# Latent attention's first weights loaded during the ternary feed-forward, its rotary exchange moved to VectorE, and the gated ternary work re-timed

## What is computed

```python
# ternary feed-forward: w -> clip(round(w / mean|w|), -1, 1)
h = gelu(x @ w1q.T + b1, approximate=False);  y = h @ w2q.T + b2
# latent attention
q = (x @ wq).reshape(b, s, H, NOPE + ROPE)      # 128 plain + 64 rotary channels a head
ckv = x @ wkv_a                                 # 128 latent channels + 64 rotary ones
q_pe, k_pe = rope(q_pe), rope(k_pe)             # re = xe*cos - xo*sin; ro = xo*cos + xe*sin
kv = (c @ wkv_b);  k = [k_nope, k_pe];  o = softmax(causal(q k^T / sqrt(192))) v
return o @ wo
# gated feed-forward, weights in bf16, groups of 64 (used two stages later)
scale = max(mean|w_g|, 1e-8);  w_hat = clip(round(w_g / scale), -1, 1) * scale
w_used = w + (w_hat - w)
```

## Time and profile before

| what | value |
|---|---|
| median of 3 runs | 2308.65 us |
| profiled execution, its own time | 2316.98 us |
| its span in the trace | 2315.2 us |
| mean granted clock of TensorE | 0.978 |
| stage of latent attention, from barrier to end | 1367.6 to 1778.9 us |

### The profile page before, as it was taken

One profiled execution on the slowest core, in us unless ns is written; L12 is line 12 of the kernel. 1 busy time (PEld: TensorE's weight loads), 2 busy tenths in 40 slices (PEclk: granted clock), 3 DMA queues, 4 the chain that ended last, 5 costly groups with the idle time before them and its releaser, 6 DMA issues. The chain is left out here.

```text
span 2315.2 us, 35594 instructions
## 1 busy us (share of the span) xinstructions
PE 2182.3 (94%) x13410; PEld 1720.5 (74%) x13410; DVE 1444.6 (62%) x3965; ACT 1172.8 (51%) x3016; POOL 465.4 (20%) x383
## 2 busy tenths in 40 slices
PE   9998999999999999999977988999899998997998
PEld 5645788888888888888866965665655884665987
DVE  2385777787778777777657435454555456883535
ACT  2153767676767676766543424453443445771222
POOL 1210212221222212221111002223232000220533
PEclk9999999999999999999998999999999998998999
DMA  6013111100111111100003023213212310003100
GB/s 243 7 64 112 37 35 38 38 16 30 37 38 38 36 36 38 37 10 26 10 1 146 1 76 123 100 64 127 80 76 99 137 52 20 2 2 147 71 1 29
DMA packets 44772, 131.94 MB, mean 57 GB/s; under 512 B 6535, under 2 KB 21671, under 8 KB 40119
## 3 DMA queue, kind: packets, MB, share of 16 engines
q1 hardware_dynamic: 32792, 108.59, 12.8%
q0 software_dynamic: 2304, 12.58, 1.3%
q10 hardware_dynamic: 9504, 8.50, 1.2%
HBM read 109.10 MB, written 20.15 MB: 56 GB/s over the span
## 5 line engine op out<-in xcount | busy, mean ns | idle before, releaser
L782 PE MATMUL psum<-qa_kv_raw,context 128*128 128x256 f32 (+1 forms) x1536 | 343.6, 380 | 0.0
L782 PEld LDWEIGHTS psum<-qa_kv_raw,context 128*128 128x128 f32 (+1 forms) x1536 | 277.2, 184 | 44.9
L768 PE MATMUL psum<-qa_w,qa_xq 128*100 128x256 bf16 (+1 forms) x3072 | 267.0, 247 | 3.1 <-PEq L60 3.1
L768 PEld LDWEIGHTS psum<-qa_w,qa_xq 128*100 128x100 bf16 x3072 | 256.1, 126 | 4.1 <-issue 4.0
L884 ACT ACTIVATE qa_prob<-psum,qa_nm 100x361 f32<-100x361 f32 x128 | 72.0, 562 | 168.3 <-DVE qa_nm L1016 168.3
L2473 ACT ACTIVATE it_prob<-psum,it_nm 100x257 f32<-100x257 f32 (+1 forms) x256 | 101.9, 412 | 42.0 <-DVE it_nm L2497 41.8
L839 PE MATMUL psum<-qa_catq,qa_o 128*128 128x400 f32 x512 | 111.9, 361 | 9.9 <-DVE X L1055 6.0
L1108 POOL TENSOR_TENSOR qa_w<-qa_w_raw,qa_w 128x768 bf16<-128x768 f32 x28 | 46.0, 1643 | 371.0 <-DVE qa_w L958 371.0
L978 DVE BATCH_NORM_STATS2 qa_st<-psum 100x6 f32<-100x128 f32 x320 | 69.7, 284 | 78.7 <-PE psum L768 78.7
L1114 POOL TENSOR_TENSOR qa_o<-qa_o_raw,qa_o 128x512 fp32r<-128x512 f32 x32 | 40.6, 1270 | 350.5 <-DVE qa_o L966 350.5
L1007 DVE TENSOR_SCALAR qa_nrm_t<-psum,qa_mv,qa_sd 100x128 f32<-100x128 f32 x320 | 107.9, 404 | 2.4
(11 more groups left out here) (355 smaller groups left out, 5013.6 us busy)
## 6 DMA issues: line engine op xcount, KB each, us to landing
qa_w_raw<-in_qa_w SPq DMA_DIRECT2D x8, 1536.0 KB, 6.7
la_gf_raw<-in_gf_w SPq DMA_DIRECT2D x16, 768.0 KB, 4.4
gf_w<-gf_ternary SPq DMA_DIRECT2D x4, 3072.0 KB, 25.4
qa_piece<-in_tf_pieces ACTq DMA_DIRECT2D x64, 128.0 KB, 2.1
qa_o_raw<-in_qa_o SPq DMA_DIRECT2D x8, 1024.0 KB, 5.1
gf_ternary<-la_gf_made POOLq DMA_DIRECT2D x8, 768.0 KB, 3.6
gf_ternary<-gf_last_made POOLq DMA_DIRECT2D x8, 768.0 KB, 3.6
context<-in_context SPq DMA_DIRECT2D x8, 722.0 KB, 12.4
```

The costliest lines, as they stand in the source:

```text
L768: mm = pe.matmul(psum[0:T, 2 + at // 512, at % 512:at % 512 + width], xq[:, kind, k, b * T:(b + 1) * T], w3[:, s, part, k, at:at + width], ...
L782: mm = pe.matmul(psum[0:rows, i // 2, (i % 2) * 256:(i % 2) * 256 + 256], ctxT[:, k, b * TC + t0:b * TC + t0 + rows], kv_raw[:, s, k, :], ...
```

## The change

1. The ternary stage's `raws` hold two quarters, not four; SP loads quarters 2 and 3 when the blocks of quarters 0 and 1 have been made. Behind them, still in this stage, SP issues the latent stage's first four loads (`LatentEarly.fetch`) into buffers that live on their own.
2. The exchange of the rotary halves is done by DVE: `turn` multiplies by cosine in one instruction and by sine in four, each of 32 partitions, reading one block of 32 and writing its neighbour; the sum becomes a difference of two SBUF tensors. `neg_swap`, the swap units and the third block of `w_a` are gone. A quad has 12 units, and rot units come at 0, 2, 6 and 8. Keys turn in the same way.
3. Set 0 and set 1 are summed and made ternary earlier in the units, and `take_scale` comes behind the unit of its own sum.
4. Joins: `join_values(0)` comes ahead of the scores, 1 and 2 behind the first two scores, 3 in batch 1, keys in batches 2 to 5. At the start keys use banks 6 and 7 in turn, the waits on the first units are spread, and the transposes come before the keys.
5. POOL does each of its two steps in three instructions of 512 columns.
6. ACT loads its table of the exponential in the units. The image and text stage uses `w_qt`, `both` and `Y` again instead of tensors of its own.

```diff
+def fetch_ternary_quarter(sp, q, raws, raw_in, a):
+    cols, rows = slice(q * F // 4, (q + 1) * F // 4), slice(q * FC // 4, (q + 1) * FC // 4)
+    sp.dma_start(raws[0][:, q % 2], a["tf_up"][:, :, cols]).then_inc(raw_in[q], 16)
+    sp.dma_start(raws[1][:, q % 2], a["tf_down"][:, rows, :]).then_inc(raw_in[q], 16)
...
-            fetch_ternary_weights(sp, raws, raw_in, a)
+            for q in range(4):
+                if q >= 2:
+                    sp.wait_ge(S_["w_ready"], (q - 1) * FC // 4)
+                fetch_ternary_quarter(sp, q, raws, raw_in, a)
+            early.fetch(sp, a)
...
+    def fetch(self, sp, a):
+        sp.dma_start(self.w_a, a["la_a"]).then_inc(self.wa_in, 16)
+        sp.dma_start(self.w_qt[:, :, :], a["la_qt"][0]).then_inc(self.keys_in, 16)
+        sp.dma_start(self.w_kt[:, :, :], a["la_kt"][0]).then_inc(self.keys_in, 16)
+        sp.dma_start(self.w_rot, a["la_rot"][0]).then_inc(self.wrot_in, 16)
...
-    prepare = {0: 0, 4: 1, 10: 2}
-    sum_after = {2: (0, 0), 4: (0, 1), 6: (0, 2), 8: (1, 0), 10: (1, 1), 12: (1, 2), 14: (2, 0)}
+    prepare = {0: 0, 2: 1, 8: 2}
+    sum_after = {2: (0, 0), 3: (0, 1), 4: (0, 2), 5: (1, 0), 6: (1, 1), 7: (1, 2), 11: (2, 0)}
     sum_beside = {1: (2, 1), 4: (2, 2)}
-    scale_after = {q + 1: xy for q, xy in sum_after.items()}
-    make_after = {7: 0, 13: 1}
+    make_after = {4: 0, 7: 1}
+    EXP_TABLE_AFTER = 9
...
-            units += [("q", i, half), ("rot" if i < 2 else "swap", i % 2, half)]
-    takes_out = {"q": "act", "rot": "dve", "swap": "dve"}
+            units += ([("rot", i, half)] if i < 2 else []) + [("q", i, half)]
+    takes_out = {"q": "act", "rot": "dve"}
...
-            for i in range(3):
+            for i in range(2):
...
+                pe.wait_ge(S_["values_in"], 32 * g + 32)
+                join_values(0, g * 8 + 4)
                 pe.wait_ge(S_["act"], g * per_quad["act"] + per_quad["act"])
-                pe.wait_ge(S_["dve"], g * per_quad["dve"] + per_quad["dve"])
+                pe.wait_ge(S_["qrot_ready"], g * per_quad["dve"] + per_quad["dve"])
...
+            def turn(raw, i, done):
+                dve.tensor_tensor(by_batch(by_cos[:, i, :]), by_batch(raw), four(cos), ALU.mult).then_inc(S_["turned"], 1)
+                for r0 in range(0, P, ROPE // 2):
+                    to, at = slice(r0, r0 + ROPE // 2), slice(r0 ^ ROPE // 2, (r0 ^ ROPE // 2) + ROPE // 2)
+                    last = dve.tensor_tensor(by_batch(by_sin[to, i, :]), by_batch(raw[at]),
+                                             sin[at, :].unsqueeze(1).broadcast_to([ROPE // 2, 4, T]), ALU.mult)
+                    last.then_inc(done, 1)
...
-                pool.tensor_tensor(diff[:, :, :], what[r][:, :, :], gw[r][:, :, :], ALU.subtract).then_inc(S_["diff_ready"], 1)
+                for y in range(3):
+                    last = pool.tensor_tensor(diff[:, y, :], what[r][:, y, :], gw[r][:, y, :], ALU.subtract)
+                last.then_inc(S_["diff_ready"], 1)
```

More of the change, by code:

```diff
@@ L1155, in before, with ternary_ffn_stage @@
     return (g, s, b - lag, n - lag) if b >= lag else (g - 1, 1 - s, b - lag + B, n - lag)
[L1162 to L1170, removed]
+def fetch_ternary_quarter(sp, q, raws, raw_in, a):
+    cols, rows = slice(q * F // 4, (q + 1) * F // 4), slice(q * FC // 4, (q + 1) * FC // 4)
+    sp.dma_start(raws[0][:, q % 2], a["tf_up"][:, :, cols]).then_inc(raw_in[q], 16)
+    sp.dma_start(raws[1][:, q % 2], a["tf_down"][:, rows, :]).then_inc(raw_in[q], 16)
+def ternary_ffn_stage(nc, core, a, abs_sums, early):
     X, psum = core.X, core.psum
@@ L1647, with __init__ @@
 LA_SCALE = float(1.0 / np.sqrt(NOPE + ROPE))
+class LatentEarly:
+    def __init__(self, nc, ctx):
+        self.both = ctx.enter_context(nc.sbuf_tensor("la_w_both", [P, 2 * C * 2 * P], F32))
+        self.w_a, self.w_rot = (self.both[:, i * C * 2 * P:(i + 1) * C * 2 * P].rearrange("p (c o) -> p c o", c=C)
+                                for i in range(2))
+        self.w_qt = ctx.enter_context(nc.sbuf_tensor("la_w_qt", [P, 4, D], F32))
+        self.w_kt = ctx.enter_context(nc.sbuf_tensor("la_w_kt", [P, 4, LORA], F32))
+        self.wa_in, self.wrot_in, self.keys_in = (nc.alloc_semaphore(f"la_{n}") for n in ("wa_in", "wrot_in", "keys_in"))
+    def fetch(self, sp, a):
[3 more added lines that the diff above has]
+        sp.dma_start(self.w_rot, a["la_rot"][0]).then_inc(self.wrot_in, 16)
 class LastGated:
@@ L1726, in latent_attention_stage @@
             "diff_ready", "made_ready")}
+        S_.update(wa_in=early.wa_in, wrot_in=early.wrot_in, keys_in=early.keys_in)
+        core.held += [early.wa_in, early.wrot_in, early.keys_in]
         block = ctx.enter_context(nc.Block())
@@ L1842, in quad @@
                     if q >= RING:
                         e, count = taken(q - RING)
-                        pe.wait_ge(S_[e], g * per_quad[e] + count)
+                        pe.wait_ge(S_[e], (g * per_quad[e] + count) * (4 if e == "dve" else 1))
                     bank = q % RING
-                    if kind in ("q", "rot"):
-                        for k in range(C):
-                            mm = pe.matmul(psum[:, bank, 0:HALF], (w_q if kind == "q" else w_rot)[:, k, i * P:(i + 1) * P],
-                                           X[:, k, cols(h)], start=(k == 0), stop=(k == C - 1))
-                    else:
-                        pe.wait_ge(S_["dve"], unit_out(g, ("rot", i, h)))
-                        mm = pe.matmul(psum[:, bank, 0:HALF], neg_swap[:, :], by_sin[:, i, :], start=True, stop=True)
+                    for k in range(C):
+                        mm = pe.matmul(psum[:, bank, 0:HALF], (w_q if kind == "q" else w_rot)[:, k, i * P:(i + 1) * P],
+                                       X[:, k, cols(h)], start=(k == 0), stop=(k == C - 1))
@@ L1946, in quad @@
                         magnitude_and_sign(g, prepare[q])
+                    if q == EXP_TABLE_AFTER:
+                        act.activation(spare[:, 2:3], core.eps[1.0], ACT.Exp)
+                joined_values(0, g * 8 + 4)
                 exps(g, 0)
+                joined_values(1, g * 8 + 5)
                 for b in range(B):
@@ L2146, in sb @@
             return ctx.enter_context(nc.sbuf_tensor(f"itp_{name}", shape, dt))
-        w = [sb(f"w{i}", [P, C, D]) for i in range(3)]
+        w = [early.w_qt, sb("w_ki", [P, C, D]), sb("w_kt", [P, C, D])]
         ctxT = sb("context", [P, RING, C, TC])
-        sq, rms, std = sb("sq", [P, C, HALF]), sb("rms", [P, 2, HALF]), sb("std", [P, N])
+        sq = early.both[:, 0:C * HALF].rearrange("p (c t) -> p c t", c=C)
+        rms, std = sb("rms", [P, 2, HALF]), sb("std", [P, N])
         spare = sb("spare", [P, 1])
```

188 lines of the change are left out of this document (85 added, 103 removed).

## The result

The changed kernel takes 2306.45 us (median of 15 runs, 2304.84 to 2310.55), the kernel before beside it 2309.88 (15 runs, 2306.97 to 2321.16): a ratio of 0.9976, 95% interval 0.9964 to 0.9987. It is faster, by 3.4 us where 16 were forecast, and so by less than the 0.5% bound.

What follows compares the result with a forecast made beforehand. TensorE, busy 94% of the span, was taken as the bound. Start 13.5, units 0.1 x 4, loops 1.05 and 1.1 made 16 us off the median 2308.65: 2293 us, own range 2287 to 2299, wide range 2279 to 2307.

Steps and rivals of the forecast that it cites:

- The start: Latent stage up to the first query unit: early loads, smaller w_a and shorter joins take 13.5 us off, between 11.5 and 14.
- 5.4 + 3.9: Start of the stage: 5.4 us off for w_a's 16 matmuls instead of 24, 3.9 off between first join and first unit.
- The units' waits: Query units: PE waits for DVE 1.65 and 2.1 us a quad; 38.5 us against 38.6, so the units give nothing.
- the meeting with POOL: Second wait of a quad: DVE's difference of two SBUF inputs is held by POOL's instruction, 0.55 us, bounds 0 and 1.17.
- units gain as well: Rival, query units: products follow after 0.49 and meet no POOL instruction, 5.8 us more off, 2287; without waits 2278; chance 0.20.
- The loops' sizes: Batch loops: seven joins instead of eight take 0.35 us off each of the first three quads, 1.1 off the fourth.
- the key joins cost little: Last two batches of the first three quads' loops: a chain of PE, ACT and DVE waits; 0.35 us off each quad.
- the term for the clock: Third quad's loop, 2.8 us over the second's by a clock fall and a POOL meeting: left even, nothing gained or lost.
- the clock eats it: Rival: eight gaps of about 2 us in four quads instead of four make the clock fall, 2302 to 2313; chance 0.22.
- the widest range given: Whole kernel: 2279 to 2307 us, leaving out the ends of the second and third rivals and the fourth.

Runs made afterwards that it cites:

- the experiment on the loads: The changed kernel with its four early loads issued at the head of the latent stage again, as before: 2310.57 us, ratio to the kernel before 0.9978.
- pool_whole: The changed kernel with GpSimd's two steps of each set in one piece again instead of three: 2316.52 us, ratio to the kernel before 1.0006.
- the clean base: The kernel before with two idle matmuls in PE's wait ahead of the scores of each quad: 2310.32 us, ratio to the kernel before 0.9975.
- the version with both edits: The changed kernel with take_scale ahead of the rot unit's products and key joins back in batches 4 to 7: 2274.8 us, ratio 0.983.
- keys late: The changed kernel with the key joins back in batches 4 to 7 of the loop: 2301.48 us, ratio to the kernel before 0.995.
- the experiment that keeps the waits and removes all falls in the stage but one: The changed kernel with idle matmuls ahead of both sums' waits (two, three) and key joins back in batches 4 to 7: 2296.31 us, ratio 0.9917.
- Fillers: The changed kernel with idle matmuls, two ahead of the sum behind unit 3, three ahead of that behind unit 7: 2303.6 us, ratio 0.9954.

## Why the prediction was wrong

**The start was right.** Forecast 13.5 us, measured 14.25: 4.78 to PE's first matmul (forecast 4.2; 4.2 by the idle time in the experiment on the loads, the rest is the stage before) and 9.47 from there to the first unit (5.4 + 3.9 = 9.3).

**The units' waits were right.** 1.65 and 2.1 us forecast, 1.67 and 2.0 (2.35 in the fourth quad) measured, released by L2000; 38.5 a quad forecast, 38.66 in the second. The 2.1 came out by two misses that cancel: the second wait was counted 0.15 short (1.5 beside 1.65, for the same chain) and the meeting with POOL 0.2 long. Products 0.57 long and 0.60 apart, and the difference longer by 0.35 where it met a third of POOL's (0.55 taken). The rule of "VectorE: DVE Perf Modes" in the Trainium skill (Two Vector instructions with no wait between them), that an instruction which starts in another quadrant than the last is held until the earlier ones have finished, agrees with the trace. So does pool_whole with the lock that "SBUF — State Buffer" (SBUF: two separate sides) in the Trainium skill describes: 2.56 us for 0.57. The rival *units gain as well* named the price of both waits together, 3.8 a quad; they were there, and it is the order of two instructions, not faster products, that took them away (4.0 a quad).

**The loops' sizes were right, the reasons in part.** Forecast 0.35 off in each of three and 1.1 in the fourth; measured against the clean base 0.44, -0.21, 0.44 and 0.55. The second and the fourth hold a fall; without it they are 0.44 (as the others) and 1.2 (29.97 to 28.75, the fourth loop of the version with both edits). The forecast counted the join that left and held that "the key joins cost little" in the last two batches. The joins of values were in fact worth 1.2 a loop (32.75 to 31.55, keys late), and the keys moved forward gave 0.76 of it back.

**The step that failed** is the term for the clock, put at nothing: "new gaps of 1.65 and 2.1 us are as good as the old one at making the clock fall. I leave it even". Even with what? The sum was read from a profile with two falls in the stage, of which the prediction saw one, and then taken off a median that is of the lower level. The kernel before with the filler, which lies at that level (2308.5 to 2311.0), has no fall from the first unit to the end of the stage; 6.5 us lie between its span and that of the profile. So there were no falls in the base that new ones could replace, and both traces of the changed kernel have them. Against the clean lengths they cost:

| where the clock falls | us |
|---|---|
| behind the second wait, first and third quad (1.64 + 1.69) | 3.3 |
| tail of the second loop (0.66) and its projection (2.31) | 3.0 |
| tail of the fourth loop (0.67) and its projection (2.3) | 3.0 |
| behind the gaps at 1767 and 1887 (1.7 + 0.7) | 2.4 |

That is 11.7 us of a miss of 2306.45 - 2293 = 13.5; most of the rest is the base, 2308.65, which lies 1.7 us under the median of the kernel with the filler (2310.32). Without the falls the changed kernel would take about 2306.45 - 11.7 = 2295 us, an estimate, and the experiment that keeps the waits and removes all falls in the stage but one takes 2296.3, with loops that are 2.3 us shorter (3 x 0.76). So the waits stand as forecast and the clock took the gain: the rival *the clock eats it*, which had 0.22, is what happened. Its price per fall, 1.75 to 2.8, nearly held: 1.65 behind a wait, 3.0 in a tail. What it missed is the place: of eight waits two brought a fall, and the larger part was lost in loop tails that the forecast had taken for harmless, and behind gaps after the stage that are as long in the kernel before and brought little or nothing there. That 2306.45 still lies inside the widest range given, 2279 to 2307, is owed to this rival and not to the sum.

**Left open:** why the clock falls at one of two equal gaps. In both traces of the changed kernel a wait of 2.0 us in the first quad and of 2.06 in the third brought a fall, one of 2.06 in the second and one of 2.35 in the fourth did not. With the keys late it was the first and the second quad, with the late loads the first, third and fourth, with waits of the same length. Fillers show that the gap is needed for it; what else is was not settled. Nor was the start tried alone without the other parts.

## What to carry to other kernels

In an in-order queue, put the short instruction that frees another engine's buffer (here 0.69 us of `take_scale`) ahead of the long work that nobody waits for (3.6 us of turn): it was worth 18 us here, more than all the parts of the change together. Before forecasting, ask whether the profile used as base holds falls of the clock, and give each gap that the change makes or moves a price of its own, at the tails too. Work that fills an end where engines wait for each other is cheap there; moved to the middle the key joins cost 0.76 us a loop, and they left an end in which the clock fell more often.

## What the runs showed of the hardware

- A fall of TensorE's clock to half speed (1.2 GHz) lasted 3 to 7 us in the stage of the changed kernel (10 in the fourth tail of the profile before) and cost 1.65 us (units, 40.3 for 38.65) to 3.0 (second loop and projection). It came behind some single gaps of 2.0 to 2.4 us and not behind others as long, and in tails in which PE was still busy for 1.3 to 1.4 of 2.0 us. Two or three matmuls of 0.67 us in each of the two waits of a quad took the falls there away.
- A VectorE instruction of 128x400 with two SBUF inputs took 0.57 us with GpSimd idle, 0.92 beside GpSimd's pieces of 512 columns, and 2.56 beside one of 1536, where it ended 0.44 us behind it.
- Three GpSimd pieces of 512 columns took 3.38 and 3.71 us (its two steps), where one of 1536 took 3.09 and 3.08.
